# Pointwise sums in four column groups, and output biases and residuals of three chunks added outside TensorE

## The reference

```
q_in = linear(x, Wq);  Q = linear(concat(q_in, conv1d(q_in, convq)), qproj)      # k alike; V = linear(x, Wv)
tau   = sigmoid(conv1x1(gelu(depthwise3(x, tau1)), tau2_w) + tau2_b)             # 16 heads x 2048
delta = sigmoid(conv1x1(gelu(depthwise3(x, del1)), del2_w) + del2_b)
scores = (Q K^T / 4) * tau[..., None] + delta[:, :, None, :]
x = layernorm(x + softmax(scores) V @ out_w.T + out_b)
x = layernorm(x + fp4(x) @ fp4(weight).T + bias)
```

## Time and profile before

| | |
|---|---|
| median of 3 runs | 1653.81 us (1650.2 to 1654.51) |
| profiled execution | 1647.78 us, of which the span of the instructions 1645.9 us |
| TensorE busy | 1603.6 us (97% of the span) |
| VectorE | 1528.9 us (93%) |
| ScalarE | 1311.8 us (80%) |
| GpSimd | 450.5 us (27%) |
| granted TensorE clock, mean | 0.993 |
| chain that ended last | PE 80%, DVE 13%, ACT 3% |

### The profile page before, as it was taken

The page is one execution under the profiler, slowest core; times in us unless marked ns, Lnnn a source line. Parts: engine busy times, 40 slices in busy tenths (PEclk is TensorE's granted clock), DMA queues, the critical chain, the costliest instruction groups (busy, mean ns, idle before and its releaser), DMA issues.

```text
span 1645.9 us, 34655 instructions
## 1 busy us (share of the span) xinstructions
PE 1603.6 (97%) x13867; PEld 718.9 (44%) x13872; DVE 1528.9 (93%) x1616; ACT 1311.8 (80%) x2375; POOL 450.5 (27%) x1189
## 2 busy tenths in 40 slices
PE   8999999999999999999999999999999999999986
PEld 6777664333333333333333333333333343433465
DVE  5789888999999999999999999999999999998887
ACT  2876837888888888888888888888888877778645
POOL 4222246222222222222223222322242222322100
PEclk9999999999999999999999999999999999999999
DMA  3376437000700060015002400331142001010312
GB/s 115 106 184 152 143 91 112 8 9 9 86 8 8 17 78 8 11 27 72 9 9 33 65 8 9 44 54 51 43 56 40 8 8 32 21 42 12 124 60 90
DMA packets 55386, 84.80 MB, mean 52 GB/s; under 512 B 14524, under 2 KB 25404, under 8 KB 53852
## 3 DMA queue, kind: packets, MB, share of 16 engines
q1 hardware_dynamic: 53368, 82.49, 24.2%
q10 hardware_dynamic: 1856, 0.09, 0.1%
HBM read 51.36 MB, written 30.67 MB: 50 GB/s over the span
## 4 chain that ended last, share of the span: by engine, by line
PE 80%; DVE 13%; ACT 3%; issue 2%; POOL 2%; DMA 1%; SPq 0%; ACTq 0%; DVEq 0%; POOLq 0%
PE ps L935 30%; PE ps L922 23%; PE ps L227 12%; DVE mx L242 9%; PE ps L691 8%; PE ps L714 2%; PE ps L705 1%; PE ps L881 1%; ACT e L1070 1%; ACT ev L1059 1%; PE ps L663 1%; DVE stats L1171 1%; PE ps L673 1%; PE ps L879 1%; PE ps L685 0%
## 5 line engine op out<-in xcount | busy, mean ns | idle before, releaser
L242 DVE TENSOR_REDUCE mx<-ps 128x2 f32<-128x1024 f32 x1024 | 1240.8, 1224 | 44.9 <-PE ps L227 31.3
L1070 ACT ACTIVATE e<-ps 128x512 f32<-128x512 f32 x2048 | 1109.6, 596 | 205.5 <-PE ps L922 164.7
L935 PE MATMUL ps<-e,v_grp 128*32 128x256 f32 x8192 | 656.0, 392 | 6.3 <-ACT ev L1059 6.1
L922 PE MATMUL ps<-q,k 52*128 52x512 f32 x2048 | 522.7, 498 | 0.4 <-PEq L361 0.4
L227 PE MATMUL ps<-k,q 50*128 50x512 f32 x2048 | 414.6, 400 | 5.9 <-DVE mx L242 5.7
L253 POOL TENSOR_SCALAR mn<-mx 128x1 f32<-128x1 f32 x512 | 182.2, 363 | 842.3 <-DVE mx L242 841.9
L922 PEld LDWEIGHTS ps<-q,k 52*128 52x128 f32 x2048 | 198.7, 183 | 425.0 <-ACT e L1070 386.0
L935 PEld LDWEIGHTS ps<-e,v_grp 128*32 128x32 f32 x8192 | 161.8, 108 | 378.7 <-issue 204.6
L227 PEld LDWEIGHTS ps<-k,q 50*128 50x128 f32 x2048 | 196.7, 187 | 19.0 <-DVE mx L242 10.6
L256 POOL TENSOR_SCALAR nm<-mn,mx 128x1 f32<-128x1 f32 x512 | 142.8, 292 | 25.2
L691 PE MATMUL ps<-x_p,m_p 128*128 128x512 f32 x576 | 142.7, 402 | 0.0
(11 more groups left out here) (140 smaller groups left out, 619.7 us busy)
## 6 DMA issues: line engine op xcount, KB each, us to landing
k<-k_parts SPq DMA_DIRECT2D x42, 256.0 KB
q<-q_parts SPq DMA_DIRECT2D x84, 128.0 KB
k_parts<-k_sp SPq DMA_DIRECT2D x16, 512.0 KB, 4.6
q_parts<-q_sp SPq DMA_DIRECT2D x16, 512.0 KB, 4.1
att<-ev SPq DMA_DIRECT2D x32, 256.0 KB
x_c<-in_x_t SPq DMA_DIRECT2D x8, 514.0 KB, 5.8
tau_r<-tau_rows SPq DMA_DIRECT2D x16, 256.0 KB
q<-nm_rows SPq DMA_DIRECT2D x256, 2.0 KB
```

Source lines behind the costliest of these rows:

```text
L242: nc.vector.tensor_reduce(mx[:, j % 2, :, jh, qt, kc], ps[:, b0:b0 + 2, :], AX.X, ALU.max).then_inc(s_free, 1)
L922: nc.tensor.matmul(ps[:, st_bank(n), :], k_set[r, g % 2, jh, kt * P:(kt + 1) * P], q_set[r, g % 2, i % NQ, jh, :], start=True, stop=True). ...
L935: last = nc.tensor.matmul(ps[32 * h:32 * (h + 1), 0, PVW * part:PVW * (part + 1)], v_grp[:, kt, h, :], e[:, x % E_BUFS, h * CH + PVW * par ...
L1070: nc.scalar.activation(e[:, x % E_BUFS, h * CH:(h + 1) * CH], ps[:, st_bank(n), :], ACT.Exp).then_inc(e_ready, 1)
```

## The change

1. **Four column groups.** Each of the four pairs of side and channel half gets its own 32 columns, `32 * (2 * c + k)`, and sums only its two r. COMBOS runs over r outermost. The half sums lie in rows 0 to 63 and 64 to 127 of the bank. ScalarE copies the upper half to `td_c` in SBUF, VectorE adds the lower half to it, and ScalarE puts one sigmoid over all 64 rows, after the next chunk's first four middle taps. `pw_b` gets 64 rows and is zeroed by GpSimd ahead of its load.
2. **Twelve tiles.** For chunks 0 to 2 TensorE does only the two matmuls with the weights. GpSimd adds the output bias (loaded once more, into `bv_bc`) to x_in, and VectorE's copy of the tile becomes an addition of x_in.
3. **GpSimd's order.** `biases` comes after iteration 0, `normalise` between the folds: chunks 0 and 1 within iteration 24, chunks 2 and 3 within iterations 28 and 29.

```diff
-        COMBOS = [(k, c, r) for c in range(CT) for r in range(2) for k in range(2)]
+        COMBOS = [(k, c, r) for r in range(2) for c in range(CT) for k in range(2)]
@@ GpSimd, projection
+                nc.gpsimd.memset(pw_b[:], 0.0).then_inc(pw_zero, 1)
@@ ScalarE, projection
+                act.wait_ge(pw_zero, 1)
                 for k, name in enumerate(("tau", "del")):
...
                     if n > 0:
+                        act.wait_ge(td_added, n)
+                    nc.scalar.activation(td_c[:], ps[64:128, TD_BANK, :], ACT.Copy).then_inc(td_copied, 1)
+                    if n + 1 < NCHUNK:
+                        middle(n + 1, range(4))
+                    act.wait_ge(td_added, n + 1)
+                    if n > 0:
                         act.wait_ge(tau_stored, 16 * n)
                         act.wait_ge(d_split, n)
-                    nc.scalar.activation(td[0:H, :], ps[0:H, TD_BANK, :], ACT.Sigmoid, bias=pw_b[0:H, :])
-                    nc.scalar.activation(td[32:32 + H, :], ps[32:32 + H, TD_BANK, :], ACT.Sigmoid, bias=pw_b[32:32 + H, :]).then_inc(td_ready, 1)
-                    if n + 1 < NCHUNK:
-                        middle(n + 1, range(4))
+                    nc.scalar.activation(td[:], td_c[:], ACT.Sigmoid, bias=pw_b[:]).then_inc(td_ready, 1)
@@ VectorE, projection, at the start of chunk n
+                    dve.wait_ge(td_copied, n + 1)
+                    if n > 0:
+                        dve.wait_ge(td_ready, n)
+                    nc.vector.tensor_tensor(td_c[:], ps[0:64, TD_BANK, :], td_c[:], ALU.add).then_inc(td_added, 1)
@@ TensorE, pointwise
                     if n > 0:
-                        pe.wait_ge(td_ready, n)
+                        pe.wait_ge(td_added, n)
                     for j, (k, c, r) in enumerate(COMBOS):
                         pe.wait_ge(gelu_done, 8 * n + j + 1)
-                        last = nc.tensor.matmul(ps[32 * k:32 * k + H, TD_BANK, :], pw_w[:, k, 2 * c + r, :], hid[:, k, c, r, :],
-                                                start=(j < 2), stop=(j >= 6))
+                        group = 32 * (2 * c + k)
+                        last = nc.tensor.matmul(ps[group:group + H, TD_BANK, :], pw_w[:, k, 2 * c + r, :], hid[:, k, c, r, :],
+                                                start=(r == 0), stop=(r == 1), skip_group_check=True)
@@ TensorE, attention (EARLY = 3)
+                        if n >= EARLY:
+                            nc.tensor.matmul(dst, ones3[:], bias3[:, 0, 0, :], start=True, stop=False)
+                            nc.tensor.matmul(dst, ident_f[:], x_in[:, p, a, :], start=False, stop=False)
@@ VectorE, attention
-                                nc.vector.tensor_copy(y_of[n][:, a], ps[:, s_bank(s), 0:D]).then_inc(s_free, 1)
+                                if a == 0:
+                                    dve.wait_ge(x_biased, n + 1)
+                                nc.vector.tensor_tensor(y_of[n][:, a], ps[:, s_bank(s), 0:D], x_in[:, n % 2, a], ALU.add).then_inc(s_free, 1)
@@ GpSimd, attention
                         nc.gpsimd.tensor_tensor(a_t[p], a_t[p], r_t[p], ALU.mult).then_inc(a_norm, 1)
+                        if n < EARLY:
+                            pool.wait_ge(bo_loaded, 16)
+                            pool.wait_ge(x_in_loaded[p], 16 * (n // 2 + 1))
+                            nc.gpsimd.tensor_tensor(x_in[:, p], x_in[:, p], bv_bc[:].unsqueeze(1).broadcast_to([P, TT, D]), ALU.add).then_inc(x_biased, 1)
...
-                    biases()
                     for group in range(FOLD_AHEAD):
                         fold(pool, 1, group)
                     for i in range(NIT):
...
+                            if i == Z_AT + 8 and c % 2:
+                                normalise(c // 2)
+                            if i in (NIT - 4, NIT - 3) and c == 1:
+                                normalise(i - (NIT - 4) + 2)
...
+                        if i == 0:
+                            biases()
@@ SP, start of the attention
+                    sp.dma_start(bv_bc[:], t["bo"].partition_broadcast(P)).then_inc(bo_loaded, 16)
```

More of the change, by code:

```diff
@@ L288, in layer_kernel @@
         k_sp = sb(early, "k_sp", [P, CT, 2, CH], F32R)
-        td = sb(early, "td", [48, CH])
+        td = sb(early, "td", [64, CH])
         d_sp = sb(early, "d_sp", [48, 2, CH], F32R)
@@ L299, in layer_kernel @@
         pw_w = sb(early, "pw_w", [P, 2, CT * 2, H])
-        pw_b = sb(early, "pw_b", [48, 1])
+        pw_b = sb(early, "pw_b", [64, 1])
+        td_c = sb(early, "td_c", [64, CH])
         w_in = sb(early, "w_in", [P, 2, CT, D])
@@ L326, in layer_kernel @@
         td_full, td_ready = sem("td_full"), sem("td_ready")
+        pw_zero, td_copied, td_added = sem("pw_zero"), sem("td_copied"), sem("td_added")
         d_high, d_split = sem("d_high"), sem("d_split")
@@ L780, in layer_kernel @@
         x_in_loaded = [sem(f"x_in_loaded{p}") for p in range(2)]
-        a_norm = sem("a_norm")
+        a_norm, bo_loaded, x_biased = sem("a_norm"), sem("bo_loaded"), sem("x_biased")
         A_INC = 16 * (HG + CT)
@@ L874, in _, with block_of @@
                 def _(pe):
-                    def block_of(dst, p, a):
-                        nc.tensor.matmul(dst, ones3[:], bias3[:, 0, 0, :], start=True, stop=False)
-                        nc.tensor.matmul(dst, ident_f[:], x_in[:, p, a, :], start=False, stop=False)
+                    def block_of(dst, n, a):
+                        p = n % 2
+                        if n >= EARLY:
+                            nc.tensor.matmul(dst, ones3[:], bias3[:, 0, 0, :], start=True, stop=False)
+                            nc.tensor.matmul(dst, ident_f[:], x_in[:, p, a, :], start=False, stop=False)
                         for c in range(CT):
-                            last = nc.tensor.matmul(dst, a_t[p][:, c, P * a:P * (a + 1)], wo_t[:, c, :], start=False, stop=(c == CT - 1))
+                            last = nc.tensor.matmul(dst, a_t[p][:, c, P * a:P * (a + 1)], wo_t[:, c, :],
+                                                    start=(n < EARLY and c == 0), stop=(c == CT - 1))
                         return last
                     def loaded(n):
-                        pe.wait_ge(x_in_loaded[n % 2], 16 * (n // 2 + 1))
                         pe.wait_ge(a_norm, n + 1)
+                        if n >= EARLY:
+                            pe.wait_ge(x_in_loaded[n % 2], 16 * (n // 2 + 1))
+                        if n == EARLY:
+                            pe.wait_ge(bias_ready, 1)
                     def s_item(s):
@@ L896, in s_item @@
                                 loaded(n)
-                            if (n, a) == (0, 0):
-                                pe.wait_ge(bias_ready, 1)
-                            block_of(ps[:, s_bank(s), 0:D], n % 2, a).then_inc(s_full, 1)
+                            block_of(ps[:, s_bank(s), 0:D], n, a).then_inc(s_full, 1)
                             return
@@ L950, in project @@
                                 pe.wait_ge(y_ready, 7)
-                        last = block_of(tok(o_bank(n), a), n % 2, a)
+                        last = block_of(tok(o_bank(n), a), n, a)
                         if a % 2:
@@ L1359, in _ @@
                         g = i // NQ
-                        if i == Z_AT + 8:
-                            normalise(0)
-                            normalise(1)
-                        if i in (NIT - 4, NIT - 3):
-                            normalise(i - (NIT - 4) + 2)
                         for c in range(4):
```

## The result

The changed kernel takes **1636.92 us** (median of 5 runs, 1631.41 to 1640.68) against 1652.64 us for the kernel before (5 runs, 1647.07 to 1654.51): ratio 0.9903, 95% interval [0.9875, 0.9931]. In a second comparison it was 1635.02 against 1649.48, 0.9917 [0.9893, 0.9942]. All ratios leave out two disturbed executions, 4545 and 2023 us, both of part 3 alone. Forecast: 1640.9, in 1633 to 1650. The profiled execution has a span of 1629.6 us, 16.3 less than the 1645.9 of before; the forecast took 12.9 off.

The account below looks back on a forecast made before the run. A ring of VectorE and ScalarE was taken to pace the projection, GpSimd's biases the seam, VectorE and TensorE in turn the tiles; -2.2 - 4.5 - 6.8 + 0.6 = -12.9 us gave 1640.9 us, range 1633 to 1650.

Parts of the forecast that it names:

- The ring: Projection chunk: VectorE and ScalarE wait on each other in a closed 25.74 us loop without pointwise sums; TensorE only follows.
- the rival that TensorE alone binds: Projection stage: TensorE is the only bound, so column groups give 14.4 us, in all 1628.7 us; chance 0.10.
- The turn: Projection, one round of VectorE and ScalarE per chunk, 25.74 us: 0.1 us shorter in each of six, 0.6 in all.
- The head: ScalarE's work from a chunk's start to the first half of k: 5.66 us becomes 5.55.
- The first chunk: Projection start: VectorE's 3.26 us wait for middle taps shrinks, only about 0.6 us coming through (0 to 1.6).
- The new joining: Joining half sums: ScalarE copy 0.60 us, one sigmoid 0.71, VectorE addition 0.68 filling its 0.72 us wait, costing nothing.
- The limit by the last gelu: Pointwise sums in chunk 4: the set cannot end before the last gelu plus 0.9 us, passing on about 0.65 us.
- The seam: Between projection and attention: moving GpSimd's biases removes the 1.32 us TensorE stall and the clock's fall, -4.5 us.
- the clock's fall: Behind the seam's stall, 7.2 us at granted clock 0.53: goes with the stall, worth 3.4 us at most.
- The tiles: Twelve out-projection tiles in the attention: 0.71 us each off TensorE, 8.5 less 1.7, so -6.8 us.
- Iteration 24: GpSimd's product and addition delay the last fold and split some 0.8 us behind VectorE's transpose, +0.6 us.
- The slower rival: Pointwise sets: TensorE waits for gelus and its clock falls, seven falls costing 24 us, in all 1665 us; chance 0.05.

Follow-up runs that it names:

- part 3 alone: Only the twelve tiles' bias and residual off TensorE and normalise between folds, against the kernel before: 1650.31 us, ratio 1.0001; second time 1649.24, 0.9994.
- half_pw: Kernel before with half of each pointwise sum left out (8 instructions instead of 16 a chunk): 1648.91 us, ratio 0.9992.
- before_off: Kernel before with only GpSimd's two subtractions of a chunk moved away from VectorE's third four taps: 1649.09 us against 1648.9, ratio 0.9995.
- part 2: Only the call of biases moved behind iteration 0, against the kernel before: 1646.73 us, ratio 0.9984.
- late_off: Changed kernel with ScalarE's sigmoid behind the second half of k and GpSimd's subtractions away from the third four taps: 1636.89 us, ratio 0.9917 to the kernel before.
- off_taps: Changed kernel with GpSimd's two subtractions of a chunk moved away from VectorE's third four taps: 1627.34 us against 1650.47 for the kernel before, ratio 0.9875.
- parts 2 and 3: Biases behind iteration 0 and the twelve tiles, without the four column groups: 1640.65 us against 1650.47 for the kernel before, ratio 0.9939.

## Why the prediction was right, and where it was not

**The ring: right, but half of the picture.** half_pw shows that in chunk 4 TensorE's saving could not pass, as forecast; the rival that TensorE alone binds (1628.7) is out. The forecast did not see that TensorE's own work was just as long, because its busy 20.00 of 20 us was put down to pacing. It cost the forecast of the time little, but it hid what part 1 was good for.

**The turn: 0.1 us forecast, 0.24 measured in chunk 4** (25.74 to 25.50) **and 0.35 on the mean.** ScalarE's heads are 0.66 us earlier in chunk 1 and 2.77 in chunk 7, so the six turns gave 2.1 us instead of 0.6. Two steps were mis-sized. The head, "5.66 - 0.71 + 0.60 = 5.55", measured 5.49 (copy and sigmoid overlap their neighbours); that is 0.06 us a turn. The larger one is "between these there is a ring without a hole", which was read in chunk 4 and taken for all chunks. The last two turns fell by 0.43 and 0.61 us (25.39 to 24.96, 25.70 to 25.09). In the kernel before VectorE waits 1.53 and 1.57 us for scores at the heads that end them, and half_pw, which takes time from TensorE alone, shortens the same turns by 0.27 and 0.59. There TensorE's saving did pass.

The first chunk: the wait for middle taps was 3.26 and is 1.99 for the second four alone, and the head of the first turn comes 0.66 us earlier (forecast 0.6). That agreement can't be leaned on, since four traces with this projection have that head at 67.64 to 68.96 us, by how long the clock fell ahead of it (last section). From it to the last table load the four traces agree, 175.3 us, and four with the old projection have 178.1: 2.8 us of part 1 are firm.

**The new joining: right.** Copy 0.60, sigmoid 0.73, addition 0.67 (forecast 0.60, 0.71, 0.68), the addition inside a wait that was there. The limit by the last gelu held: the set ends at 161.66 + 3.37 = 165.03, 1.1 us behind the gelu (forecast at least 0.9).

**The seam: right in mechanism; its size holds for an execution in which the clock falls.** In the pair of traces it is -4.7 against -4.5. But the clock did not fall each time. half_pw and before_off have the old seam, with stands of 1.17 and 1.45 us on TensorE, and behind them the granted clock is 1.00, here in half_pw and then in before_off:

```profile
283.40:293.40 10.00, 9.99 (x96) 3.86 (x98) 9.96 (x9) 7.55 (x15) 2.49 (x8) 1.00 0.03 8
```

```profile
286.70:296.70 10.00, 10.00 (x96) 3.87 (x98) 9.97 (x9) 7.56 (x14) 2.51 (x8) 1.00 0.02 3
```

From the last table load to the third transpose they take 74.6 and 74.9 us, where the kernel before took 77.6 and those with part 2 take 73. So part 2 is worth some 4.5 us in an execution with the fall and 1.5 to 2 without it, and the 3.0 us of its medians lies between. How often the fall comes is not known, as each kernel has one trace. The step "so does the clock's fall" took it as certain. That the sum came out for the whole is in part luck: with parts 1 or 3 in, the stall to be removed is no longer the 1.32 us of the earlier trace rows but 2.5 or 3.1 us, with a longer fall. What part 2 is worth once the other two are in was not run; if parts 1 and 3 give 4 to 5 us together, as alone, the whole (14 to 16 us) leaves some 10 for it.

**The tiles: right sum, wrong step.** "12 x 0.71 = 8.5, less 1.7" gave 6.8; measured 6.1. But a plain tile passes only 11.59 - 11.13 = 0.46 us (VectorE's tiles 1344.86 to 1356.45 before, 1335.16 to 1346.29 after). Of the 0.28 us of the bias matmul, 0.27 came back as 1.13 - 0.86 on the out-projection: the first matmul of the item pays the start, whoever it is. Twelve such tiles are 5.5 us, not 8.5, and the deduction of 1.7 for tiles without waits happened to cover most of that. Over all traces, the stretch between the two stores takes 277.1 to 283.4 us in the six with the old tiles and 271.1 to 277.2 in the seven with the new ones, 5.7 us less on the mean. And VectorE's second wait, 0.42 us, never could go, since the item after the tile starts no earlier against the tile.

**Iteration 24: right**, 0.66 us of wait for GpSimd (forecast 0.8), +0.5.

**The rest, -1.7 us** in the tail, is no gain of the change. From the last of these stores to the end the profiled execution of before takes 67.4 us, and every other trace 65.4 to 65.8, those of the kernels with the old tiles too. The execution of before was slow there.

**The slower rival** did not come: in chunk 4 the granted clock is 1.00 although TensorE's sums go at the gelus' pace. Its "it decides from a stand of about 1.3 us" is not borne out either: a stand of 1.45 us passed without a fall, and two of 0.71 and 0.53 us had one behind them (last section).

## What to carry over

A busy engine and a closed ring can be two limits of one length: take time from each alone, then from both, before either is written off. Price an item by what the stretch between two equal items loses, not by the removed rows, since the first instruction of what is left takes over the start. And an engine that nobody waits for still costs where it works beside another: GpSimd's idle 70% was free, its 2.2 us beside VectorE's taps were not. And a difference between two traces is a difference of two executions: where the clock falls in one and not in the other, look for a third.

## What the runs showed of the hardware

**VectorE beside GpSimd.** Four taps (two SBUF inputs each) take 2.73 us alone, 4.18 us with GpSimd's work of 0.60 + 1.62 us beside them, 4.53 with 2.00 (late_off), 5.92 us with 2.77 + 1.62. GpSimd can pay too: with no taps beside them its subtractions take 2.40 and 1.29 us, wholly beside the taps 2.77 and 1.62. Maxima from PSUM beside the same subtraction keep their length (2 in 2.35 us). The Trainium skill, "SBUF — State Buffer", section "SBUF: two separate sides", says that a VectorE operation with two SBUF inputs and a GpSimd operation that reads SBUF lock each other out of a shared port pair for a whole instruction. The trace agrees in kind. In size it does not: by an estimate from that page's rule, full blocking would make 2.73 + 2.22 = 4.95 and 2.73 + 4.39 = 7.12 us, and 4.18 and 5.92 were measured.

**The granted clock.** It fell after short stands in the attention, too. In off_taps TensorE stands 0.71 us and 0.53 us within 3 us, and the stretch from 1374 us shows 0.59:

```profile
1372.66 0.50 PE L227 MATMUL ps<-k,q 50*128 50x512 f32 x2 [0.71 <-DVE mx L242]
...
1374.92 2.08 PE L898 MATMUL ps<-wo_t,v_all 128*128 128x256 f32 x4 [0.53 <-DVE mx L242]
```

```profile
1374.00:1378.00 4.00, 3.47 (x18) 1.44 (x14) 2.90 (x5) 1.37 (x3) 1.46 (x5) 0.59 0.46 138
```

The same out-projection takes 2.08 us there instead of 1.13, and the iteration 47.3 instead of 46.3. But the same stands pass without a fall elsewhere. The changed kernel has them too (0.67 and 0.51 us at 1378 and 1381 us), the kernel before as well (0.66 and 0.52 at 1389 and 1392), and both keep a clock of 1.00 there; both also keep it behind a stand of 1.45 us in a later iteration, near 1450 and 1464 us, behind which (1.48 us, at 1445) off_taps is at 0.80. So the length of a stand does not tell by itself whether the clock falls: it differs between executions. Kernels with old tiles and with new ones show one to three such falls among the tiles, the profiled executions of before, after and part 2 none.

And it fell where TensorE was never idle: behind 32 matmuls of one column each (L696, 50.8 to 54.9 us in the kernel after) it is at the lower level, 1.2 GHz:

```profile
50.00:55.00 5.00, 5.00 (x37) 4.83 (x37) 3.01 (x6) 4.96 (x7) 0.00 (x0) 0.87 0.03 7
55.00:60.00 5.00, 5.00 (x18) 4.44 (x19) 4.86 (x8) 3.15 (x4) 4.24 (x3) 0.50 0.77 216
```

Such a fall, in one or both of the places where these matmuls run, is in every profiled execution, and its length differs from one to the next; this is why ScalarE's head of chunk 1 comes up to 5 us later in some profiles (parts 2 and 3: 73.66 us against 68.68) whatever was edited.
